# Two-layer GNN: layer 1's edge list is coded, counted and ranked between layer 0's first 176 gathers, the feature table is written in seven batches while x is still loading, and 18 instead of 16 list columns are placed per 16 gathered chunks

## The reference, cut to what matters

```python
def layer0(x, src, dst):                       # GraphSAGE-like
    agg = segment_sum((x @ W_l.T + b_l)[src], dst, 6250)
    deg = segment_sum(1, dst, 6250)
    return agg / max(deg, 1)[:, None] + x @ W_r.T
def layer1(h, src, dst):                       # gathers by dst, sums by src
    neigh = segment_sum(h[dst] @ W_neigh.T + b_neigh, src, 6250)
    neigh = neigh / max(segment_sum(1, src, 6250), 1)[:, None]
    o = h + relu(h @ W_self.T + b_self + neigh)
    return layernorm(o) * gamma + beta
x = layernorm(x + layer0(x, src, dst))
x = layernorm(x + layer1(x, src, dst))
```

## Time and profile before

| | |
|---|---|
| median of 3 runs | 2965.13 us (2956.29 to 2967.65) |
| the profiled execution | 2964.21 us, span of the trace 2962.5 us, 1.7 us outside it |
| busy share of the span | PE 79%, DVE 76%, POOL 66%, ACT 47% |
| head, to the first gather | 147.7 us |
| layer 0's gathers, first to last | 147.7 to 1344.7 us |

### The profile page before, as it was taken

How to read it: one execution, slowest core, us unless ns; L and a number is a source line. 1 busy time by engine, 2 the same in 40 slices (tenths; PEclk the granted TensorE clock), 3 DMA queues, 4 the chain that set the end, 5 groups by cost and what they waited for, 6 DMA issues and landing times.

```text
span 2962.5 us, 53780 instructions
## 1 busy us (share of the span) xinstructions
PE 2333.3 (79%) x9888; PEld 1014.9 (34%) x9888; DVE 2242.3 (76%) x4956; ACT 1402.1 (47%) x3557; POOL 1953.1 (66%) x2021
## 2 busy tenths in 40 slices
PE   3288988898999989887886677777777777776996
PEld 1133444444444444433332232223222323222443
DVE  6899888888888888886876666666665666654998
ACT  3501555656555555553344443443443443442776
POOL 0277777777777777772112777777777777775775
PEclk8699999999999999999998989888898898875998
DMA  5577777777877777775456888888888888878676
GB/s 202 174 203 230 229 225 226 234 229 235 236 223 234 231 222 232 232 214 148 148 162 210 247 244 252 249 242 252 248 244 249 250 241 252 248 218 182 226 241 202
DMA packets 247012, 664.11 MB, mean 224 GB/s; under 512 B 39593, under 2 KB 40423, under 8 KB 246949
## 3 DMA queue, kind: packets, MB, share of 16 engines
q0 software_dynamic: 144640, 475.92, 56.6%
q1 hardware_dynamic: 101828, 186.19, 18.5%
q10 hardware_dynamic: 480, 1.28, 0.2%
HBM read 573.26 MB, written 89.97 MB: 224 GB/s over the span
## 4 chain that ended last, share of the span: by engine, by line
PE 37%; DVE 19%; DMA 19%; issue 13%; POOL 5%; DVEq 4%; ACT 1%; POOLq 0%; SPq 0%; ACTq 0%
PE ps L1139 36%; DMA rows<-table,idx_ring 16%; POOL rows L542 4%; DVE acc L897 3%; DVE acc L977 3%; DVE onehot L884 2%; DVEq L891 2%; DVE where L909 2%; POOL rows L526 1%; DMA table<-rows 1%; DMA g_idx<-table,idx_ring 1%; DVE flat L1094 1%; DVE flat L1047 1%; DVE st L1051 1%; DVE flat L1049 1%
## 5 line engine op out<-in xcount | busy, mean ns | idle before, releaser
L1139 PE MATMUL ps<-rows,onehot 128*128 128x512 f16 (+1 forms) x4104 | 896.3, 335 | 365.8 <-DMA rows<-table,idx_ring 172.9
L526 POOL DMA_INDIRECT rows<-table,idx_ring x928 | 894.4, 964 | 309.3 <-issue 211.8
L977 DVE TENSOR_TENSOR acc<-acc,ps 128x513 f32 x880 | 606.4, 689 | 440.9 <-PE ps L1139 301.1
L1139 PEld LDWEIGHTS ps<-rows,onehot 128*128 128x128 bf16 x4104 | 371.6, 102 | 933.5 <-issue 220.3
L542 POOL DMA_INDIRECT rows<-table,idx_ring x440 | 422.9, 961 | 150.5 <-issue 95.4
L1139 PE MATMUL ps<-where,put 128*128 128x440 bf16 x1664 | 451.0, 353 | 37.9 <-DVE where L909 36.6
L1139 PE MATMUL ps<-w_b,flat 128*128 128x512 f32 x784 | 470.1, 684 | 0.0
L909 DVE TENSOR_SCALAR where<-iota_chunk,cw_ring 128x880 bf16<-128x880 f16 x832 | 428.1, 515 | 8.6 <-PE ps L1139 1.7
L1448 ACT ACTIVATE put<-spot,flat 128x128 f16<-128x128 f16 x832 | 265.7, 390 | 337.5 <-PE ps L1139 330.2
L1436 ACT ACTIVATE spot<-iota_node,flat 128x128 f16<-128x128 f16 x832 | 340.4, 479 | 125.5 <-DVE flat L753 125.5
L897 DVE TENSOR_TENSOR acc<-acc,ps 128x513 f32 x464 | 318.3, 686 | 97.1 <-PE ps L1139 55.1
(11 more groups left out here) (236 smaller groups left out, 2335.4 us busy)
## 6 DMA issues: line engine op xcount, KB each, us to landing
table<-rows SPq DMA_DIRECT2D x98, 257.0 KB, 3.7
rows<-table,idx_ring POOLq DMA_INDIRECT x1368, 3.9
xr_scratch<-edges SPq DMA_DIRECT2D x49, 256.0 KB
rows<-xr_scratch SPq DMA_DIRECT2D x49, 256.0 KB, 3.2
h_scratch<-rows SPq DMA_DIRECT2D x49, 256.0 KB, 2.1
flat<-h_scratch SPq DMA_DIRECT2D x49, 256.0 KB, 5.1
hb_scratch<-spot SPq DMA_DIRECT2D x49, 256.0 KB, 4.1
u_scratch<-flat SPq DMA_DIRECT2D x49, 256.0 KB
```

The lines of the kernel that those rows point to most:

```text
L526: nc.gpsimd.indirect_dma_start(out=rows[:, k % GB, :], out_offset=None, in_=tables[layer][:, :], in_offset=bass.IndirectOffsetOnAxis(ap=id ...
L977: V.tensor_tensor(tile_acc, tile_acc, part, ALU.add).then_inc(s_acc, 1)
L1139: return nc.tensor.matmul(*args, skip_group_check=True, **kw)
```

## The change

1. **Listing.** `bin_starts(1)`, `bin_rank(1)` and `places(1)` become one generator, `listing`, of 161 steps; PE's part becomes the generator `listed`. Layer 0's first LISTING = 11 iterations take one step before each chunk: 18 steps of coding, 2 for the bins, 25 for the masks (two a step), 10 for counts, scan, starts and chunk tiles, 98 for the ranks (a rank, then a mask), the rest for the places. That is 176 chunks. Nothing of layer 1's list is left in the head or in a run of its own. Counts and their reads move to PSUM banks 0 to 2.
2. **Table.** x comes in seven batches of seven tiles (SP issues the last two behind the stores of table batches 0 and 1). ACT finds the maxima of batches 0 to 5, DVE those of batch 6; scales, high halves, low halves and tails go batch by batch, over 14 slots: seven in `rows`, seven in the weights' place (`spare`). ACT's copy of the identity for `pick` shrinks from 49x6272 to 49x49 elements and is read with stride 0 as a matmul's weights.
3. **Placing.** PC = 18 columns per 16 chunks, the two extra at chunks 7 and 15, in 46 iterations; the last iteration places 4 columns and carries four x products (at chunks 0, 4, 8 and 12) and three transposes (at chunks 2, 6 and 10). `spot` and `put` get a third buffer of four columns.

The core of the diff, first the constants and SP:

```diff
+        PC = 18
+        BODIES = (EC - 1) // (2 * PC)
+        LAST_COLS = EC - 2 * BODIES * PC
+        LISTING = CHUNKS[0] // U - 2 * BODIES - 1
+        w_ab = sb("w_ab", [P, 2, KC, D], f32)
+        pick = sb("pick", [T, T], f16)
+        stage = [rows[:, k, :] for k in range(BATCH)] + [spare[:, k * TW:(k + 1) * TW] for k in range(BATCH)]
...
+            for b in range(5):
+                x_batch(b)
+            table_batch(0)
+            x_batch(5)
+            table_batch(1)
+            x_batch(6)
+            for b in range(2, T // BATCH):
+                table_batch(b)
```

DVE in the head:

```diff
+            scales(0)
+            scales(1)
+            lows(0)
+            scales(2)
+            lows(1)
             dve.wait_ge(s_win, 1)
...
+            scales(3)
...
-            bin_starts(1)
...
             hand_over(0, 0, 0)
+            lows(2)
+            scales(4)
+            lows(3)
+            scales(5)
+            lows(4)
+            scales(6)
+            lows(5)
+            lows(6)
             dve.wait_ge(s_low, T)
             V.memset(acc[:, ACT_CLEARS * BATCH:T, :], 0.0).then_inc(s_zero, T // BATCH - ACT_CLEARS)
```

DVE's `listing` and `chunks`:

```diff
+                link(V.tensor_scalar(inta, other, 1, None, ALU.arith_shift_right))
+                yield
...
+                for b in range(T):
+                    make_mask(s, b, b)
+                    if b % 2 == 1:
+                        yield
...
+                for b in range(T):
+                    dve.wait_ge(s["used"], T + b + 1)
+                    if b:
+                        dve.wait_ge(s["max"], b)
+                    at = 2 * (b % RB[1])
+                    V.tensor_tensor(pos.rearrange(halves, h=2), pos.rearrange(halves, h=2), ps[:, at:at + 2, 0:HC],
+                                    ALU.max).then_inc(s["max"], 1)
+                    yield
+                    if b + MB < T:
+                        make_mask(s, T + b + MB, b + MB)
+                    yield
...
+                    if lister is not None:
+                        next(lister, None)
                     if place is not None:
-                        spread(place, k, isinstance(place, int) and place == 0)
+                        for j in range(k * cols // U, (k + 1) * cols // U):
+                            spread(place, j, half, isinstance(place, int) and place == 0)
                     hot(layer, i, k, first and layer == 0)
-                    if rank and k % g == g - 1:
-                        bin_rank(1, AHEAD + RIDE * i + k // g)
...
+                    if last and k % 4 == 3:
+                        x_evict(T - 4 + k // 4, (T - 4 + k // 4) % 2)
```

PE's `sums` and its loop, then ACT in the head:

```diff
+                    if lister is not None:
+                        next(lister, None)
...
+                    if last and k % 4 == 0:
+                        for j in range(KC):
+                            x_product(T - 4 + k // 4, j)
+                    if last and k % 4 == 2 and k < 12:
+                        x_turn(T - 3 + k // 4, (T - 3 + k // 4) % 2)
...
+                    with pe.Fori(1, BODIES) as c:
+                        for k in range(2):
+                            sums(0, 2 * c + k + LISTING, placing=2 * c + k, turn=2 * c + k, product=2 * c + k - 1, half=k)
+                    sums(0, iters - 1, last=True, placing=2 * BODIES)
...
+            bounds(0)
+            for b in range(1, DVE_MAXIMA):
+                bounds(b)
+                highs(b - 1)
+            for b in range(DVE_MAXIMA - 1, T // BATCH):
+                highs(b)
+            for b in range(ACT_CLEARS):
+                clear(b)
```

More of the change, by code:

```diff
@@ L927, in add_beta, with chunks @@
                 V.tensor_tensor(hbout, hin, vec[4], ALU.add).then_inc(s_lhb, 1)
-            def chunks(layer, i, first=False, last=False, place=None, rank=False, side=None, half=0):
+            def chunks(layer, i, first=False, last=False, place=None, lister=None, side=None, half=0):
                 g = GROUP[layer]
+                cols = LAST_COLS if last else PC
                 for k in range(U):
@@ L1000, in _ @@
                     dve.wait_ge(s_zero, 7)
[L1001 to L1007 removed]
+                    lister = listing()
+                    for i in range(LISTING):
+                        chunks(0, i, first=(i == 0), lister=lister)
+                    for _ in lister:
+                        pass
+                    chunks(0, LISTING, place=0)
+                    chunks(0, LISTING + 1, place=1, side=0, half=1)
+                    with dve.Fori(1, BODIES) as c:
                         for k in range(2):
[L1009 to L1011 removed]
+                            chunks(0, 2 * c + k + LISTING, place=2 * c + k, side=2 * c + k - 1, half=k)
+                    chunks(0, iters - 1, last=True, place=2 * BODIES)
                 else:
@@ L1256, in side_product, with sums @@
                     last.then_inc(s_lproj, 1)
-            def sums(layer, i, first=False, placing=None, rank=False, turn=None, product=None, half=0):
+            def sums(layer, i, first=False, last=False, placing=None, lister=None, turn=None, product=None, half=0):
                 g = GROUP[layer]
+                cols = LAST_COLS if last else PC
                 for k in range(U):
+                    if lister is not None:
+                        next(lister, None)
                     if placing is not None:
-                        place(1, U * placing + k, k, start=(isinstance(placing, int) and placing == 0 and k == 0),
-                              stop=(isinstance(placing, int) and placing == EC // U - 1 and k == U - 1))
-                    if rank and k % g == 0:
-                        rank_bin(1, AHEAD + RIDE * i + k // g)
+                        for j in range(k * cols // U, (k + 1) * cols // U):
+                            place(1, PC * placing + j, PC * half + j, put_at=(PC * half + j) // PB % 3,
+                                  start=(isinstance(placing, int) and placing == 0 and j == 0), stop=(last and j == cols - 1))
                     q = k // g
@@ new lines, in _, with puts @@
+            for b in range(ACT_CLEARS):
+                clear(b)
+            def puts(c, g):
+                s, col, at = lists[1], 2 * PC * c + PB * g, PB * (g % 3)
+                first = isinstance(c, int) and c == 0 and g < 3
+                if not first:
+                    act.wait_ge(s["put"], col - 2 * PB)
+                for k in range(PB):
+                    last = nc.scalar.activation(spot[:, at + k, :], iota_node[:], ACT.Abs,
+                                                scale=value[:, ds(col + k, 1)], bias=shift_v[:, ds(col + k, 1)])
+                last.then_inc(s["spot"], 1)
+                made = PC // 2 * c + g + 1
+                free = col - 2 * PB
+                if not isinstance(made, int):
+                    made, free = act.to_reg(made), act.to_reg(free)
+                act.wait_ge(s_code, 1)
+                act.wait_ge(s["spot"], made)
+                if not first:
+                    act.wait_ge(s["placed"], free)
+                for k in range(PB):
+                    nc.scalar.activation(puts_of[g % 3][:, k, :], spot[:, at + k, :], ACT.Relu, scale=-1.0,
+                                         bias=value[:, ds(col + k, 1)]).then_inc(s["put"], 1)
```

498 lines of the change are left out of this document (274 added, 224 removed).

## The result

The changed kernel takes 2935.19 us (median of 5 runs, 2929.46 to 2937.99) against 2961.61 for the kernel before beside it (5 runs): a ratio of 0.9907, 95% interval 0.9886 to 0.9928. It is faster by 26 us; the forecast was 2930. The profiled execution has a span of 2933.4 us, 29.1 under the 2962.5 of before.

What follows compares the result with a forecast made beforehand. Layer 0 bound by POOL's gathers, DVE and PE close behind. 94.0 + 220.4 + 6 + 46 x 21.0 + 15 x 1.2526 + 5.5 = 1310.7 against 1344.7, -34.0, giving 2930 us; range 2903 to 2960.

Steps and rivals of the forecast that it cites:

- The head: Before the first gather: listing leaves and the table goes in batches, first gather from 147.7 to 94.0, 53.7 us earlier.
- last low half to first gather was 4.9 us: End of the table build: the earlier trace's 4.9 us interval kept, taking 89.1 to a first gather at 94.0.
- the +1.3 us: Late table stores: full DMA engines would carry a tile in 0.76 us, worth +1.3 us on 14 tiles.
- The listing: 176 chunks beside layer 0's gathers: 220.4 us at POOL's pace plus 6 us lost, between 2 and 15.
- DVE's bunch of ten steps: Listing, counts to chunk tiles: 19 us of DVE work against 12.5, with eight gather buffers absorbing some.
- The coding and the masks: Listing on DVE: coding 26 us against 25 in 20 chunks, masks 0 to 3 us over in 25 chunks.
- DVE's run of places: Early layer 0: said to precede the 4.8 us lateness of gather number 100-odd, and to go with the change.
- `pick` with stride 0: Listing's ranks on PE: reading these weights with stride 0 might cost 0 to 5 us; taken as 0.
- The placing: 46 iterations of 18 columns: +0.38 us each over 20.62, so 21.0 us per iteration.
- Rival 1: Placing: two columns are free, 20.6 us per iteration stays, 18 us less, 2912 us; chance 0.20.
- The last iteration: End of placing: 25.3 us of PE against 20.0, so +5.5 us with hand-overs; late last x store covered.
- rival 3: PE stays at 1.2 GHz in the listing: +114 us, 3044; in part +22, 2952; chance 0.12, a quarter the whole.

Runs made afterwards that it cites:

- spreading alone: The changed kernel with eight empty steps put between the ten heavy listing steps from counts to chunk tiles: 2929.83 us, ratio 0.9899.
- filler alone: The changed kernel with unread 512-column matmuls on PE, one per coding chunk, three per chunk in the ten steps: 2930.96 us, ratio 0.991.
- all three edits together: The changed kernel with eight empty listing steps, unread matmuls on PE and the last x load split in two: 2918.45 us, ratio 0.9884.

## Why the prediction came out right, point by point

- **The head** (-53.7 forecast, -49.7 measured). The last low half ended at 89.8 (forecast 89.1), and that is partly luck. ACT's maxima take 0.61 us each here instead of 0.75, which is some 6 us less over 42 tiles; and ACT waits 7.1 us for landed stores, of which the forecast had none ("14 slots take away the waits"). The longest of these waits:

```profile
69.58 2.72 ACT L1560 ACTIVATE rows<-acc,inv 128x512 f16<-128x512 f32 x4 [4.20 <-DMA table<-rows]
```

  The store that it waits for could not go out before 57.98, since DVE stood at its branch from 49.0 to 57.0. So the pause, 8.0 us instead of 3.86, was not covered, though the head's working says that it is. The step that failed is "last low half to first gather was 4.9 us": the interval was taken over from a stage with the DMA engines at 0.81, and the +1.3 us that the working names for full engines is not in its sum; with them at 0.92 (66 to 94 us) it took 8.2. A store landed after 6.7 us in the median, after 3.7 before. The first one-hot, which the zeroing sets, came at 102.15 (100.5).
- **The listing** (226.4 forecast, 244.15 measured, beyond the 2 to 15 us of its range). The forecast priced DVE's bunch of ten steps rightly (19 against 12.5 us) and then let the eight buffers absorb it. They didn't: PE hangs on the same DVE, waits, drops to 1.2 GHz, and enters the ranks late and slow. The ten steps' two iterations lost 13.6 us; spreading alone gave 8.6 back, filler alone 4.9. The coding and the masks (26 against 25 us, and 0 to 3 over) lost 6.4 us in the first three iterations; PE is at 0.50 in the coding, but the filler, which raised that, gave nothing back there. Another 2.4 us lie in the last iteration, most of them the weights' transfers. The forecast had seen this gap in the earlier trace rows and put it down to DVE's run of places, which it said would go; the runs show that in the new place the transfers cause most of it. In the old place both coincided: in this row of before DVE is busy 4.83 of 5 us and the DMA share is 1.01, so the earlier trace rows could not tell them apart.

```profile
280.00:285.00 5.00, 2.80 (x9) 1.13 (x10) 4.83 (x15) 4.81 (x14) 0.27 (x1) 0.50 1.01 378
```

- **`pick` with stride 0**: no cost is seen; four of the ranks' iterations take 20.06 to 20.13 us, as in the earlier trace rows; the one of 21.22, which all of the new form have at 20.4 to 21.7 on the faster cores, was not looked into.
- **The placing** (21.0 forecast, 20.46 measured). Here the working was wrong: it read 0.58 us over POOL's pace as a price of load, and scaled it with the load. Nearly half of it in before (12 us in 44 iterations, 0.28 each) is rare gaps, most of them with PE at 1.2 GHz, which more load on PE makes fewer; the rest is spread over all iterations, and grew by 0.1 us. Rival 1, two columns free, is what happened (chance 0.20), and the pitch fell by 0.1 us besides: fewer gaps, against a longer median iteration.
- **The last iteration** (+7.7 over forecast). PE's 25.3 us were about right: with the load split (all three edits together), four of its chunks take 1302.78 - 1296.58 = 6.20 us, so sixteen 24.8. What was missed is a transfer: the last x tile's load, which in before went out at 1262.3 and was first used at 1284.98, and was on no path; here it is needed at once. The claim that the late end is covered by the vectors' load was wrong too: the loads are issued behind it, so `rdeg` and the next stage (DVE at 1333.49 against 1362.29) both came 29 us earlier, no more and no less.
- **The clock.** Coding ran at 0.50 and the ten steps at 0.63, the ranks at 0.99: rival 3 in part, but not at its price. Of the 17.7 us that the listing is over the forecast the filler, which lifts the ten steps to 0.85, gives back 5.1. The Trainium skill, "TensorE: Matmul & The Clock Gate", section "HAM oscillation — how this bites in real kernels", describes this, and the trace agrees in kind; but with DVE's steps spread a clock of 0.80 or 1.00 made no difference (235.8 and 237.0 us).
- **The sum.** 4.5 us off at the end of layer 0 is +4.0 +17.7 -24.9 +7.7. The total was near by luck: the free columns of rival 1 paid for the listing, whose loss the prediction had put at 6 us and took to be absorbed beyond that.

## What to carry to other kernels

A steady loop's excess over its bound should be looked at gather by gather before it is scaled: as far as it is a few long gaps, it need not grow with the work per turn, and here the gaps became fewer. Compare loops over stretches that hold the same work: 0.07 us per iteration of the first comparison came from one odd iteration. When work is moved beside a loop, lay it out by the longest step, not by the sum; buffers between engines don't help when the engine behind them waits for the same overloaded one. And list every transfer that the moved code issues or needs at its new place: here a load of 106 rows, two of 1 MB and five vectors each became the thing waited for.

## What the runs showed of the hardware that was not expected

- A load of 106 rows of 2 KB took some 10 us to land, one of 128 rows 4.4 to 4.8, and as 96 and 10 rows it was waited for by nobody.
- In the placing loop PE with more work spent less time at 1.2 GHz: 44 and 41 us of 900 with 16 columns, 10 with idle matmuls added to them, 9 with 18 columns, 30 with two of the 18 made thin.
- Two transfers of 1 MB beside gathers filled the DMA engines (0.98 and 1.04 over 10 us, up to 400 GB/s), and PE stood for 4.4 us; in eight pieces its longest wait there was 1.7 us.
- DVE's pause at a branch that skips a long block was 3.8 to 4.1 us in four profiles, and 7.3 to 10.1 in nine with other code around it, 8.00 and 10.08 in the same kernel on two cores.
- One core paused all its engines for some 1.6 us every 9.3 us in the placing, and not in the head, which made the same program 17% slower.
